# A two-layer graph network on one core: 32 of the 80 basis loads combined among the z and mix products

## What is computed

```python
w = jnp.einsum('rb,bio->rio', att, basis)          # 2 relations from 30 bases of 512 x 512, twice
x_j = x[col]
for r in range(NUM_RELATIONS):
    gate = jax.nn.sigmoid(x_j @ gate_w[r, :, 0])
    msgs.append(gate[:, None] * x_j @ w[r])
msg = jnp.where((edge_type == 0)[:, None], msgs[0], msgs[1])
agg = jax.ops.segment_sum(msg, row, num_segments=x.shape[0])
return agg + x @ root + bias                       # layer 1, relu, then layer 2
...
qkv = x @ W_qkv                                    # the mix: 8 heads
out = jnp.einsum('bhnd,bhde->bhne', q_phi, KV) / denom
```

## Time and profile before

| | us |
|---|---|
| median of 3 runs | 1010.71 |
| lowest, highest | 1009.82, 1012.64 |
| span of the profiled execution | 1014.3 |
| PE busy in it | 945.3 (93%) |
| DVE, ACT, POOL busy | 556.8, 400.6, 109.6 |

### The profile page before, as it was taken

The page is one execution under the profiler, slowest core; times in us unless marked ns, Lnnn a source line. Parts: engine busy times, 40 slices in busy tenths (PEclk is TensorE's granted clock), DMA queues, the critical chain, the costliest instruction groups (busy, mean ns, idle before and its releaser), DMA issues. The chain is left out here.

```text
span 1014.3 us, 12428 instructions
## 1 busy us (share of the span) xinstructions
PE 945.3 (93%) x4724; PEld 612.8 (60%) x4724; DVE 556.8 (55%) x1176; ACT 400.6 (39%) x670; POOL 109.6 (11%) x98
## 2 busy tenths in 40 slices
PE   3789889799999999999999899989999899999998
PEld 1245445257454476458775655889998644445885
DVE  5588887742227541334212772498777643558871
ACT  3467775331111211111111332468786553423550
POOL 0000000000020023100002000144331000022300
PEclk9899999799999999998999999999999999999899
DMA  8888988852000102016595400513101300230001
GB/s 305 281 341 332 336 325 343 321 196 90 0 14 6 51 3 83 1 46 233 199 319 187 172 0 1 172 43 84 43 1 44 123 1 3 87 83 0 1 2 50
DMA packets 53039, 124.87 MB, mean 123 GB/s; under 512 B 5408, under 2 KB 19492, under 8 KB 52963
## 3 DMA queue, kind: packets, MB, share of 16 engines
q1 hardware_dynamic: 51314, 121.46, 33.9%
q0 software_dynamic: 1120, 1.29, 0.5%
q10 hardware_dynamic: 528, 1.05, 0.3%
HBM read 120.40 MB, written 3.38 MB: 122 GB/s over the span
## 5 line engine op out<-in xcount | busy, mean ns | idle before, releaser
L409 PE MATMUL PS<-AR 128*125 128x512 f32 (+9 forms) x1394 | 394.0, 440 | 9.0 <-issue 1.9
L409 PEld LDWEIGHTS PS<-AR 128*128 128x128 f32 (+3 forms) x1394 | 212.5, 194 | 169.0 <-issue 161.9
L442 PE MATMUL PS<-AR 128*32 128x512 f32 x576 | 88.2, 628 | 35.4 <-DMA AR<-in_basis 34.4
L1949 ACT ACTIVATE AR<-PS 128x500 f32<-128x500 f32 (+6 forms) x73 | 41.9, 578 | 167.3 <-PE PS L409 81.5
L1952 ACT ACTIVATE AR<-iota,AR 125x625 f16<-125x625 f16 x119 | 86.1, 810 | 39.1 <-PE PS L495 38.9
L442 PEld LDWEIGHTS PS<-AR 128*32 128x32 f32 x576 | 19.4, 111 | 91.0 <-issue 56.2
L1278 DVE TENSOR_SCALAR AR<-iota,AR 125x625 f16<-125x625 f16 x165 | 60.5, 442 | 17.6 <-PE PS L495 17.6
L493 PE MATMUL PS<-AR 125*125 125x512 f16 (+9 forms) x425 | 61.2, 302 | 3.5 <-issue 3.4
L493 PEld LDWEIGHTS PS<-AR 125*125 125x125 f16 x425 | 46.2, 142 | 21.7 <-issue 12.3
L2447 POOL TENSOR_TENSOR whl<-AR,whh 128x512 fp32r<-128x512 f32 x32 | 47.8, 1513 | 89.8 <-ACT whh L1949 89.8
L1797 DVE TENSOR_TENSOR HMl<-AR,HMh 128x626 fp32r<-128x626 f32 x64 | 51.3, 841 | 4.6 <-ACT HMh L1949 4.6
(11 more groups left out here) (318 smaller groups left out, 1479.1 us busy)
## 6 DMA issues: line engine op xcount, KB each, us to landing
AR<-in_basis SPq DMA_DIRECT2D x80, 768.0 KB, 8.3
AR<-in_L_ffn_W SPq DMA_DIRECT2D x20, 1024.0 KB, 7.8
AR<-in_L_gnn_Wh SPq DMA_DIRECT2D x8, 512.0 KB, 4.0
AR<-in_L_gnn_Wh SPq DMA_DIRECT2D x16, 256.0 KB, 4.7
AR<-in_L_mix_W_qkv SPq DMA_DIRECT2D x1, 3072.0 KB, 11.3
AR<-in_L_gnn_root SPq DMA_DIRECT2D x2, 1024.0 KB, 14.7
y_dram<-AR SPq DMA_DIRECT2D x8, 256.0 KB, 8.1
AR<-in_WkvT SPq DMA_DIRECT2D x1, 2048.0 KB, 8.6
```

The source lines that it names most:

```text
L409: ins = te.matmul(o, l, r, start=start and i == 0, stop=stop and i == len(pairs) - 1)
L442: ins = te.matmul(CB[32 * j:32 * j + 32, :], Am[:, l, m, 16 * (n % 2):16 * (n % 2) + 32], ring[:, at // 3, at % 3, :], start=m == quarter[ ...
L1949: return se.activation(o, i, ACT.Copy, scale=scale)
```

## The change

- The order of the bases is no longer by groups but by loads. `bases(a, b)` replaces `combos` and takes loads a to b - 1, each with the column parts that its three tiles serve (`PART_OF`), and frees its buffer by itself. `LOADS` says which loads follow which segment: 48 loads (0 to 47) under the 24 segments, two or three at a time. Loads 48 to 54 stand between three root products, 55 to 61 between the z products, 62 to 79 between and within the q, k and v products.
- From load 50 on the ring has three buffers; the other two take W_k and W_v (`Wkv0`), issued behind load 57. W_q goes into the place of the normalised x and is issued when `gx_low` is through (`gxl_ready`); it stands in SP's list ahead of load 58.
- CB's bank also takes the five transposes of x (`turn0`), one after each of the segments 2, 5, 8, 11 and 14; ScalarE copies all five out, and the next group waits for that (`xt0_read`).
- The statistics and scaling of x come after the first segments' rows instead of before; the masks `Am` are built by GpSimd instead of VectorE; SP issues edges and iota first.
- The fourth root product moves to `layer1(3)`, the held banks are those of slots 0 and 3, and the flags are summed before x is touched. VectorE's one-hot rows are 628 wide instead of 625.

```diff
-FREES = (2, 5, 8, 11, 17)
-AFTER = [g // 2 + 2 if g % 2 else None for g in range(NS)]
...
+WID = 628
...
+LOADS = {0: (0, 2), 1: (2, 5), 3: (5, 8), 4: (8, 10), 6: (10, 13), 7: (13, 15), 9: (15, 18), 10: (18, 20), 12: (20, 23),
+         13: (23, 25), 15: (25, 28), 16: (28, 30), 17: (30, 33), 18: (33, 35), 19: (35, 38), 20: (38, 40), 21: (40, 43),
+         22: (43, 45), 23: (45, 48)}
+GROUP_AT = {g: b // 5 - 1 for g, (_, b) in LOADS.items() if b % 5 == 0}
+TURN_AT = {2: 0, 5: 1, 8: 2, 11: 3, 14: 4}
+PART_OF = ((0, 3), (3, 6), (6, 9), (9, 12), (12, 18))
...
+def ring_at(n):
+    return (n % 5, n // 5 + 1, n - 5) if n < 50 else ((n - 50) % 3, 11 + (n - 50) // 3, n - 5 if n < 53 else n - 3)
...
+        Wq0, Wkv0 = ar(oXN, 4, 512), ar(oR2 + 4608, 4, 1024)
...
-        bank = [PS[0:P, 512 * c:512 * c + 512] for c in range(4)]
+        bank = [PS[0:P, 512 * k:512 * k + 512] for k in (0, 1, 6, 7)]
+        home = (0, 0, 3, 3)
...
-            def combos(n, a=0, b=len(PARTS)):
-                l = n // 8
-                pe.wait_ge(w_ready, n)
-                for m, (c, j) in list(enumerate(PARTS))[a:b]:
-                    at = ORDER.index(c)
-                    pe.wait_ge(d_ring[at // 3], 16 * (n + 1))
-                    quarter = [k for k, part in enumerate(PARTS) if part[1] == j]
-                    ins = te.matmul(CB[32 * j:32 * j + 32, :], Am[:, l, m, 16 * (n % 2):16 * (n % 2) + 32],
-                                    ring[:, at // 3, at % 3, :], start=m == quarter[0], stop=m == quarter[-1])
-                    if m in FREES:
-                        ins.then_inc(combo_done, 1)
+            def bases(a, b):
+                for n in range(a, b):
+                    g, j = n // 5, n % 5
+                    l, (slot_, use, _) = g // 8, ring_at(n)
+                    if n == 0:
+                        pe.wait_ge(am_ready, 6)
+                    if j == 0:
+                        pe.wait_ge(w_ready, g)
+                        pe.wait_ge(xt0_read, min(NT, g))
+                    pe.wait_ge(d_ring[slot_], 16 * use)
+                    for m in range(*PART_OF[j]):
+                        c, q = PARTS[m]
+                        quarter = [k for k, part in enumerate(PARTS) if part[1] == q]
+                        ins = te.matmul(CB[32 * q:32 * q + 32, :], Am[:, l, m, 16 * (g % 2):16 * (g % 2) + 32],
+                                        ring[:, slot_, ORDER.index(c) % 3, :], start=m == quarter[0], stop=m == quarter[-1])
+                    ins.then_inc(combo_done, 1)
+            def turn0(c):
+                pe.wait_ge(d_cst, 16)
+                pe.wait_ge(w_ready, c + 1)
+                pe.wait_ge(xn_ready, LN_X + c + 1)
+                for k in range(4):
+                    ins = te.transpose(CB[:, k * P:(k + 1) * P], XN[0:P, c, k * 128:(k + 1) * 128], ident[0:P, 0:P])
+                ins.then_inc(xt0_full, 1)
...
-            pe.wait_ge(am_ready, 6)
-            combos(0)
...
-            pe.wait_ge(d_cst, 16)
-            for c in range(NT):
-                pe.wait_ge(xn_ready, LN_X + c + 1)
-                turn(("xt", 0, c), c, XN, 4, "dve" if c % 2 else "act")
-            combos(1)
...
-                if AFTER[g]:
-                    combos(AFTER[g])
+                if g in LOADS:
+                    bases(*LOADS[g])
+                if g in TURN_AT:
+                    turn0(TURN_AT[g])
...
-                    te.matmul(o, XT[:, k, cols(c)], (R1e if c < 4 else R1)[:, k, :], start=k == 0, stop=False)
+                    te.matmul(o, XT[:, k, cols(c)], (R1e if c < 3 else R1)[:, k, :], start=k == 0, stop=False)
...
-            psum.held.update((0, 1))
-            combos(14, 0, 6)
-            pe.wait_ge(d_r1e, 16)
+            psum.held.add(0)
+            psum.at = 1
+            bases(48, 50)
+            pe.wait_ge(d_r1, 16)
             for s, v in psum.free[0]:
                 pe.wait_ge(s, v)
             root1(0, bank[0])
-            combos(14, 6, 12)
+            bases(50, 52)
             root1(1, bank[1])
-            combos(14, 12)
-            u = psum.take("many", "dve", slot=2)
+            bases(52, 54)
+            root1(2, bank[2])
+            bases(54, 55)
+            u = psum.take("many", "dve")
             slot(u)
             pe.wait_ge(many_ready, 1)
             te.matmul(sl(u.slot, 0, 10, 1), ones[0:P, 0:1], sm[0:P, 3, 0:2, 0:5], start=True, stop=True).then_inc(u.sem, 1)
-            root1(2, bank[2])
-            combos(15, 0, 6)
-            root1(3, bank[3])
-            combos(15, 6)
-            psum.held.discard(3)
...
+                    i = 4 * r + kc
+                    if i < 5:
+                        bases(55 + i, 56 + i)
+                    elif i > 5:
+                        bases(54 + i, 55 + i)
...
+            def mix_kv(L, c, XT, between=()):
...
+                    if j == 0 and between:
+                        bases(*between)
...
+                u = psum.take(("l1", c), "act", slot=home[c] if c < 4 else None)
                 o = bank[c] if c < 4 else sl(u.slot, 0, 512, P)
                 if c == 4:
                     slot(u)
-                    pe.wait_ge(d_r1, 16)
+                if c > 2:
+                    pe.wait_ge(w_ready, 16)
+                    pe.wait_ge(d_r1, 32)
                     root1(c, o)
...
-            pe.wait_ge(d_wqkv, 16)
-            for m in range(4):
+            pe.wait_ge(d_q, 16)
+            for m, (a, b) in enumerate(((62, 64), (64, 65), (65, 67), (67, 69))):
                 mix_q(0, m, XT)
-            for c in range(NT):
-                mix_kv(0, c, XT)
+                bases(a, b)
+            pe.wait_ge(d_kv, 16)
+            for c, (a, b, e) in enumerate(((69, 70, 70), (70, 72, 74), (74, 75, 75), (75, 77, 78), (78, 79, 80))):
+                mix_kv(0, c, XT, (a, b))
+                bases(b, e)
             for r in range(2):
                 for kc in range(4):
...
-            dv.wait_ge(d_att, 32)
-            for lay in range(2):
-                for k in range(3):
-                    ve.tensor_tensor(Am[:, lay, :, 16 * k:16 * k + 16], amask,
-                                     att[:, :, lay, k % 2].unsqueeze(2).to_broadcast([128, 18, 16]),
-                                     ALU.mult).then_inc(am_ready, 1)
...
-            dv.wait_ge(d_x, 16)
-            for c in range(NT):
-                ln_stats(X, 512, c)
-                if c:
-                    ln_scale(X, c - 1, LN_X + c)
-            ln_scale(X, NT - 1, LN_X + NT)
+            def ends(g):
+                if g > 1:
+                    dv.wait_ge(seg_done, g - 1)
+                for t in range(*SEGS[g]):
+                    ve.tensor_scalar(oh_dst(g, t)[:, 0:WID], iota[0:P, 0:WID], ef[:, 1, t:t + 1], ef[:, 2, t:t + 1],
+                                     ALU.is_equal, ALU.mult).then_inc(dst_ready, 1)
+                for t in by_dve(g):
+                    ve.tensor_scalar(oh_src(g, t)[:, 0:WID], iota[0:P, 0:WID], ef[:, 0, t:t + 1], None,
+                                     ALU.is_ge).then_inc(src_dve, 1)
+            dv.wait_ge(d_iota, 16)
+            ends(0)
...
+            dv.wait_ge(d_x, 16)
+            for c in range(NT):
+                ln_stats(X, 512, c)
...
+                if g == 0:
+                    for c in range(NT):
+                        ln_scale(X, c, LN_X + c + 1)
+                if GROUP_AT.get(g, 0) % 2:
+                    combo_in(GROUP_AT[g])
+                if 0 < g <= NT:
                     dv.wait_ge(d_gw0, 16)
-                    dv.wait_ge(xn_ready, LN_X + g + 1)
...
-            ends(1)
+            def turned0(c):
+                ac.wait_ge(xt0_full, c + 1)
+                copy(XT[:, :, cols(c)], CB[:, 0:500].rearrange("p (k n) -> p k n", k=4)).then_inc(xt0_read, 1)
...
+                if g == 0:
+                    for c in range(NT):
+                        ln_root(c, LN_X + c + 1)
+                if GROUP_AT.get(g, 1) % 2 == 0:
+                    combo_out(GROUP_AT[g])
+                if g in TURN_AT:
+                    turned0(TURN_AT[g])
...
+            po.wait_ge(d_att, 32)
+            for lay in range(2):
+                for k in range(3):
+                    ge.tensor_tensor(Am[:, lay, :, 16 * k:16 * k + 16], amask,
+                                     att[:, :, lay, k % 2].unsqueeze(2).to_broadcast([128, 18, 16]),
+                                     ALU.mult).then_inc(am_ready, 1)
...
+            ye.dma_start(ei, A["edges"]).then_inc(d_edge, 16)
+            ye.dma_start(iota[:, :], A["c_iota"]).then_inc(d_iota, 16)
             ye.dma_start(amask, A["c_amask"]).then_inc(d_att, 16)
             ye.dma_start(att, A["att"]).then_inc(d_att, 16)
-            ye.dma_start(ei, A["edges"]).then_inc(d_edge, 16)
-            ye.dma_start(iota[:, :], A["c_iota"]).then_inc(d_iota, 16)
...
-                r = n % 5
-                if n > 4:
-                    sp.wait_ge(combo_done, n - 4)
+                r, _, before = ring_at(n)
```

(7 more changed lines are left out.)

91 lines of the change are left out of this document (39 added, 52 removed).

## The result

The changed kernel takes 1032.97 us (median of 4 runs, 1030.67 to 1035.32) against 1010.27 us of the kernel before (1007.91 to 1012.64): ratio 1.0222, 95% interval 1.0193 to 1.0251. It is 22.7 us slower, where 1008.8 us and a range of 1001 to 1018 us were forecast.

The account below looks back on a forecast made before the run. Basis loads, waiting for ring buffers that TensorE frees five at a time, bound the front part. Pieces -35.9 - 1.4 + 32.5 + 2.9 = -1.9 us on the 1014.3 us span, carried over 0.4% lower: 1008.8 us, range 1001 to 1018.

Parts of the forecast that it names:

- Piece A: Adjacency, until its last segment ends: 141.5 us instead of 177.4, 35.9 us less.
- the second cycle: Second six adjacency segments: VectorE 27.2 us, TensorE 25 us, 30.8 us with the waits from segment to segment.
- rival (3): Adjacency segments: costlier hand-overs or GpSimd port share, TensorE's low clock deciding; kernel slower, 1019 us, chance 0.15.
- The start: Before the adjacency: edges land at 3.8 us, flags at 12.2 us instead of 25.5, GpSimd's masks cost VectorE 2 us.
- Piece B: From the last adjacency segment to the first z product: 39.9 us instead of 41.3.
- z's slow start: First z products at half clock rate after TensorE's idle time: 2.5 us, counted in Piece B.
- Piece C: z and mix products: 107.4 us, 32.5 us more than 74.9, from 30 rounds and 19 switches.
- rival (4): Loads behind the wait for the split x come late, TensorE waits between z products; 1013 us, chance 0.10.
- The price of a switch: Among z and mix products: switching to 32-column products and back costs 0.34 us, 6.5 us for 19 bursts.
- Piece D: Everything behind z and mix products: fourth root product +3.4 us, small waits -0.5 us, +2.9 us in the sum.
- rival 1: VectorE's one-hot rows become faster by the new width, three cycles x 3 us = 9 us: 1000 us, chance 0.08.

Follow-up runs that it names:

- e5: Changed kernel with one more product of zeros behind each of the seven restart products of the second, third and fourth cycle: 1039.78 us, ratio 1.0292.
- e2: Changed kernel with three of its 48 loads behind each of segments 5 and 11, where banks are flushed, other bursts and turns moved: 1027.40 us, ratio 1.0175.
- e12: e7's kernel with each group's products in two bursts of nine, one behind each segment, instead of one of 18: 1013.74 us, ratio 1.0033.
- e6: Changed kernel with first-layer root weights issued when segment 21 is closed instead of 23, third root product behind the flag product: 1020.92 us, ratio 1.0097.
- e3: Changed kernel without the products of loads 55 to 79, except one 8-column product a load; loads and waits stay: 1035.83 us.
- e10: Changed kernel with the 25 loads behind z in 10 bursts of two or three loads instead of 19 bursts: 1026.55 us, ratio 1.0167.
- e1: The kernel before, unchanged, run and profiled once more: 1008.55 us, profiled span 1007.4 us.
- e8: As e6, but 60 loads by segment 23, 5 among the root products and 15 behind z: 1013.34 us, ratio 1.0019.
- e4: Changed kernel's start and fine cut, but all 80 loads before the first z product, ring of five buffers throughout: 1011.55 us, ratio 1.0014.
- e7: Kernel before with only edges and iota issued first and the masks built by GpSimd: 1009.42 us, ratio 0.9988.
- e9: As e4, but loads spread evenly, a burst of three or two loads behind every segment: 1010.97 us, ratio 1.0004.
- e11: As e4, with the first five loads issued ahead of x and the constants: 1011.02 us, ratio 0.9995.

## Why the prediction was wrong, point by point

**Piece A is the step that failed** (141.5 us forecast, 159.4 measured). The prediction took VectorE and ScalarE, with the hand-overs between the engines, for the limit (30.8 us for the second cycle) and gave TensorE 25 us of it, nearly 6 us of slack. TensorE in the second cycle of the changed kernel:

```profile
57.16 3.54 PE L514 MATMUL PS<-AR 125*125 125x399 f16 x14
...
60.64 2.76 PE L465 MATMUL PS<-AR 128*32 128x512 f32 x18
63.33 2.09 PE L514 MATMUL PS<-AR 125*125 125x399 f16 x14
...
71.28 3.96 PE L514 MATMUL PS<-AR 125*125 125x399 f16 x28 [0.33 <-ACT AR L1979]
...
84.52 0.17 PE L516 MATMUL PS<-zer 125*125 125x8 f16 x1
```

It is solid from 57 to 84.5 us but for two gaps of 0.15 and 0.33 us. VectorE and ScalarE wait for its segments each time:

```profile
60.75 2.57 DVE L1283 TENSOR_SCALAR AR<-iota,AR 125x628 f16<-125x628 f16 x7 [0.71 <-PE PS L516]
...
65.47 2.57 DVE L1283 TENSOR_SCALAR AR<-iota,AR 125x628 f16<-125x628 f16 x7 [0.78 <-PE PS L516]
```
```profile
65.47 3.65 ACT L1979 ACTIVATE AR<-iota,AR 125x625 f16<-125x625 f16 x5 [1.07 <-PE PS L516]
```

From the first restart to the next cycle's first (52.84 to 86.89 us) TensorE's second cycle is 34.1 us. Against the 25 us forecast for it, the segments are 15.5 us instead of 12 (1.9 of it by term 1 below, 1.5 by term 2), the restarts 4.3 instead of 1.7, the bursts 10.8 instead of 11.2, and two things were not in the sum: two turns of x, 1.3 us, and waits, 2.2 us, of which 1.7 stand before the first restart.

By stage, these are the terms beyond the forecast's cycles, 18.2 us in all (0.3 of it is my rounding from 141.2 to 141.5; the flushes end at 55.6, 89.7 and 124.9 us where 51.8, 82.6 and 113.3 were forecast):

1. **Segments that meet two column blocks, 8.1 us.** "A segment is 2.0 us, 2.5 us from segment 19 on" is false for segments 4, 9, 14 and 18: their products are issued for two blocks. 3.96 us stands above for segment 9 (x28 instead of x14), three times 1.9 us more, and segment 18 takes 4.4 us, 2.4 more. This was there to be read in the first profile of before:

```profile
64.73 4.01 PE L493 MATMUL PS<-AR 125*125 125x512 f16 x28
...
150.47 4.39 PE L493 MATMUL PS<-AR 125*125 125x173 f16 x35 [0.26 <-issue]
```

The page of before has it in one line, 61.2 us for 24 segments, 2.55 us each, where the prediction's figures add up to 49.5 us (19 x 2.0 + 4 x 2.5 + 1.5):

```profile
L493 PE MATMUL PS<-AR 125*125 125x512 f16 (+9 forms) x425 | 61.2, 302 | 3.5 <-issue 3.4
```

2. **The low clock behind each flush, 5.6 us.** Windows of the changed kernel (columns as in e5), the first flush, the segment behind it, and the one after; the last line is the third flush:

```profile
52.00:57.00 5.00, 3.77 (x7) 1.16 (x7) 5.00 (x10) 5.00 (x8) 0.00 (x0) 0.63 0.14 51
57.00:61.00 4.00, 4.00 (x20) 2.90 (x23) 3.26 (x11) 0.93 (x3) 0.00 (x0) 0.60 0.00 0
61.00:66.00 5.00, 5.00 (x41) 2.49 (x36) 4.22 (x13) 3.92 (x6) 0.00 (x0) 1.00 0.65 220
...
126.00:134.00 8.00, 8.00 (x45) 5.34 (x47) 2.47 (x8) 0.97 (x2) 0.00 (x0) 0.63 0.37 152
```

The first segments took 3.54, 3.57 and 7.06 us instead of 2.09, 2.09 and 4.4. The kernel before has whole groups of 4.5 us between a cycle's last segment and the restarts, and at two of its three flushes the seven restarts then run in one go (1.72 us, clock not lowered behind them; at the other, three restarts are paced and the next segment takes 3.39 us). In the changed kernel there is no burst at segments 5 and 11, TensorE waits 1.7 us for the flush and is then paced by it at 0.72 us a restart. e2 with a burst of three loads there has this in the same place, at the full clock:

```profile
54.00:58.00 4.00, 3.33 (x15) 1.65 (x15) 4.00 (x10) 3.72 (x6) 0.00 (x0) 1.00 0.92 358
```

The third flush costs the most, 2.7 of the 5.6 us, and there the missing burst is not the reason. A burst of three loads stands directly ahead of it, and still the restarts are paced and the clock falls:

```profile
119.78 2.76 PE L465 MATMUL PS<-AR 128*32 128x512 f32 x18
122.47 0.72 PE L504 MATMUL PS<-AR 1*125 1x512 f16 x2
...
126.32 7.06 PE L514 MATMUL PS<-AR 125*125 125x173 f16 x35
```

It falls in the same place in e2 (5.99 us) and e12 (7.25 us). Only filled restarts (e5, 4.35 us) or a whole group of 4.5 us ahead (before, 4.39 us) kept it up there in the runs shown here. Yet paced restarts alone do not decide it: behind e12's first two flushes, paced likewise behind a burst of 2.77 us, the next segment took 2.1 us.

The prediction priced the low clock as a rival (3), for waits of "over 3 us" and "from two such segments a cycle". It came once a cycle, behind flushes whose longest wait was 1.7 us, and cost 5.6 us where that rival has 12. The Trainium skill (TensorE: Matmul & The Clock Gate, Part 1: The HAM clock gate) ties the clock to how busy TensorE has been lately; the flushes agree, since each fall at one of them stands behind a wait of 1.7 us or restarts with holes of 0.3 us between them, and e5's third flush, with neither, has none.

3. **The shared bank.** The first turn of x waited until ScalarE had copied group 0 out of the bank, behind a table load and a segment's rows (TensorE, then ScalarE, of the changed kernel):

```profile
34.77 0.62 PE L475 MATMUL PS<-cst,AR 125*128 125x125 f32 x4 [2.64 <-issue]
35.49 3.24 PE L514 MATMUL PS<-AR 125*125 125x512 f16 x14
```
```profile
33.42 1.24 ACT L1976 ACTIVATE AR<-PS,cst 128x512 f32<-128x512 f32 x2
```

The segment behind it was slow too. The first cycle was 3.8 us late in all, 1.9 us beyond term 1. Later the copied x was waited for once more, 1.84 us at 108 us, and a segment's rows 0.93 us at 152 us. Terms 1 to 3 are 18.4 us. That they meet the 18.2 us so closely is partly luck: they are TensorE's, and the 30.8 and 30.7 us of the second and third cycle were not TensorE's sum. In the third cycle they are 0.7 us too much, in the fourth 0.6 us too little. The start itself was right: GpSimd's mask products cost VectorE 1.9 us (4.45 us for its first seven rows instead of 2.57), where 2 were taken, and the flags stood at 14.1 us, 12.2 and those 2:

```profile
5.49 5.07 POOL L2435 TENSOR_TENSOR AR<-AR 128x288 f32<-128x288 f32 x6 [3.18 <-DMA AR<-in_att]
...
6.99 4.45 DVE L1283 TENSOR_SCALAR AR<-iota,AR 125x628 f16<-125x628 f16 x7
```

**Piece B** was 3.1 us shorter than forecast, 2.5 of it by bookkeeping: the forecast counts z's slow start here, and the measured stretch ends where z begins. The root weights came 13.5 us behind the last segment (12 forecast), and the flag product stood at 30.6 us (31.7); the clock at z was low, as forecast. Its size was right within 1 us, and e6 shows that 7.9 us of it were not needed.

**Piece C** was right, 33.7 us more than before against 32.5. Of the 33.7 us about 1.8 are z's slow start (its first unit with a burst took 4.8 us, the second 3.1); e6, without it, has 31.8 us more than before. A q unit, a burst and a q unit of the changed kernel:

```profile
230.04 4.58 PE L426 MATMUL PS<-AR 128*128 128x512 f32 x16
234.55 1.91 PE L465 MATMUL PS<-AR 128*32 128x512 f32 x12
236.39 4.58 PE L426 MATMUL PS<-AR 128*128 128x512 f32 x16
```

No wait for a load stood behind z, so rival (4) did not come. The price of a switch (0.34 us) holds by e3 (0.34) and e10 (3.2/9 = 0.35).

**Piece D** was 718.5 us against 716.7. Against e1 it is 6.6 us longer: 3.4 us are the root product; the rest lies in what executions differ by (e2, e6, e8 and e10, with the same code there, have 714 to 717 us).

**The width** (rival 1): seven rows of 628 take 2.57 us. No effect, as costed.

**What it comes to.** Rival (3) named the side and 1019 us, but its cause, hand-overs, was not it, and the clock only in part: TensorE's own work and the shared bank were the rest. The mechanism of the loss is in the busy time. Moved loads do not vanish from TensorE: behind z each of the 25 costs 33.7/25 = 1.35 us, or 31.8/25 = 1.27 us by e6. Ahead of z they give back less: where TensorE is solid, a load can give back no more than its own products there, 2.76/3 = 0.92 us in a burst of three (an estimate), and not the 2.5 us of DMA time that the prediction saw in before. With e4's, e8's and the changed kernel's 73, 60 and 48 loads by segment 23, the last segment closes at 178.5, 168.3 and 159.4 us, 0.7 to 0.8 us a load. (The three differ in smaller things too.) The times follow: 0, 15 and 25 loads behind z give 1011.6, 1013.3 and, with early roots, 1020.9 us. The cut into bursts costs a further 1.0 us a group (e12). The early start, some 20 us, is eaten by all this, and no version beat the kernel before: e4, e7, e9 and e11 lie within 0.2% of it.

Open: why the medians of e2, e6 and e10 all fell by about 3 us more than their stretches up to the bias product (3.9, 3.1 and 3.0 us), though the code behind it is the same; and what exactly lowers TensorE's clock in a flush, since neither the wait ahead of it nor the paced restarts decide it alone.

## What to carry to other kernels

Before moving work away from a place where an engine waits, add up that engine's own rows over one whole period of the loop, odd iterations included; the wait is the most that can be had, and here other waits and the cost of cutting and switching took it all. A burst that looks like filler may be cover: see what stands in each wait (here a flush) before taking it out. And take the difference of a profile's span to its own execution's time, not to the median of others: one profile can be a long one.

## What the runs showed of the hardware

- Products with 32 weight columns run side by side: 18 in one burst take 4.49 us and 9 take 2.77. One after the other, at 0.855 us each, they would take 15.4 and 7.7 us, so 3.4 and 2.8 run at once on average (an estimate), and a cut group takes longer. The Trainium skill (TensorEngine Tiling (Array Packing), Theoretical Speedup) gives up to four times for a dimension of 32 or less; the long burst comes near it.
- Once its clock falls, TensorE pays for several us: behind waits of 1.7 us and restarts at 0.72 us steps the granted clock was 0.60 for 4 us (above), and more products in that stretch did not prevent it (e5, first two flushes). Behind a burst, with no wait, the same fill did: 4.35 instead of 7.06 us for the next segment (e5, third flush).
- VectorE's 16-bit rows took 0.64 us each instead of 0.37 beside GpSimd's products (4.45 us for seven against 2.57).
